# Two-layer convolution kernel: the low parts of x1 shared by GpSimd and VectorE, key sums moved ahead of the lane products, two x1 loads of the last stage issued earlier

## The reference, cut to what matters

```
layer 0: keys, queries, values = 1x1 convolutions of x
         context = softmax(keys over pixels) @ values ;  x1 = Wp(context, softmax(queries)) + x
layer 1: qkv  = w_qkv @ x1                       (768 channels = 32 heads x (q, k, v) x 8)
         agg  = 5x5 depthwise, then 8x8 pointwise convolution of qkv
         for both qkv and agg, per head:  q = relu(q), k = relu(k), v1 = [v, 1]
             vk  = v1 @ k^T over the pixels (9 x 8) ;  out = vk @ q ;  out = out[:8] / out[8]
         y    = w_proj @ out
         out  = batchnorm(y over all 8 images) * gamma + beta + x1
```

## Time and profile before

| | us |
|---|---|
| median of 3 runs | 2250.73 (2247.62 to 2252.7) |
| the profiled execution | 2251.85 |
| its span | 2250.1 |
| PE / DVE / ACT / POOL busy | 2059.1 / 1423.8 / 867.5 / 646.4 |
| layer 1 ends, last stage begins | 2146.3 |
| last stage | 103.8 |

### The profile page before, as it was taken

How to read it: one execution, slowest core, us unless ns; L and a number is a source line. 1 busy time by engine, 2 the same in 40 slices (tenths; PEclk the granted TensorE clock), 3 DMA queues, 4 the chain that set the end, 5 groups by cost and what they waited for, 6 DMA issues and landing times. The chain is left out here.

```text
span 2250.1 us, 33698 instructions
## 1 busy us (share of the span) xinstructions
PE 2059.1 (92%) x13448; PEld 1517.5 (67%) x13448; DVE 1423.8 (63%) x2052; ACT 867.5 (39%) x1841; POOL 646.4 (29%) x511
## 2 busy tenths in 40 slices
PE   8999999999897999999999999999999999999810
PEld 7888898888774666666666666766766666666500
DVE  6667776677248765948667575684857659480452
ACT  5444544444443423423433342343334234234142
POOL 1223312231324422522522242252243226221000
PEclk9999999999998999999999999999999999999855
DMA  3220122210677756764865776586486667647588
GB/s 124 85 85 17 69 85 85 85 74 12 232 268 267 250 199 239 261 225 172 288 230 203 266 265 210 194 292 216 167 303 237 209 238 252 228 172 263 237 340 373
DMA packets 144475, 450.91 MB, mean 200 GB/s; under 512 B 7744, under 2 KB 106688, under 8 KB 120000
## 3 DMA queue, kind: packets, MB, share of 16 engines
q1 hardware_dynamic: 143168, 429.89, 53.6%
q10 hardware_dynamic: 1152, 18.87, 2.0%
HBM read 273.95 MB, written 174.78 MB: 199 GB/s over the span
## 5 line engine op out<-in xcount | busy, mean ns | idle before, releaser
L791 PE MATMUL cv<-work,wc 128*64 128x288 f32 x4608 | 622.3, 415 | 15.9 <-issue 12.0
L1153 POOL TENSOR_TENSOR wc<-taps 128x512 f32<-128x512 f32 x288 | 366.3, 1299 | 499.4 <-PE cv L791 492.0
L791 PEld LDWEIGHTS cv<-work,wc 128*64 128x64 f32 x4608 | 308.3, 137 | 258.9 <-issue 51.5
L1233 DVE SCALAR_TENSOR_TENSOR spun<-work,spun 128x1152 f32<-128x1152 f32 x240 | 379.0, 1584 | 0.0
L1227 DVE STREAM_SHUFFLE spun<-work 128x1152 f32<-128x1152 f32 x240 | 347.9, 1456 | 0.1
L1015 ACT ACTIVATE work<-cv 128x288 f32<-128x288 f32 x384 | 157.6, 410 | 475.3 <-PE cv L791 473.6
L770 PE MATMUL pj<-x1hi,w1hi 128*128 128x288 f32 x768 | 237.3, 309 | 29.2 <-issue 24.3
L993 ACT COPY work<-pj 128x288 f32<-128x288 f32 x384 | 154.1, 401 | 232.4 <-PE pj L772 232.4
L772 PE MATMUL pj<-x1hi,w1lo 128*128 128x288 f32 x768 | 230.2, 300 | 0.0
L771 PE MATMUL pj<-x1lo,w1hi 128*128 128x288 f32 x768 | 229.0, 298 | 0.0
L420 POOL TENSOR_TENSOR qs<-qs,qrc 128x512 f32<-128x512 f32 x72 | 75.2, 1049 | 402.1 <-DVE qrc L474 402.1
(11 more groups left out here) (128 smaller groups left out, 3406.0 us busy)
## 6 DMA issues: line engine op xcount, KB each, us to landing
work<-scratch_padded SPq DMA_DIRECT2D x48, 1306.0 KB, 6.9
scratch_padded<-work SPq DMA_DIRECT2D x48, 1300.0 KB, 6.2
work<-scratch_padded SPq DMA_DIRECT2D x48, 1299.5 KB, 9.9
scratch_phases<-work SPq DMA_DIRECT2D x96, 576.0 KB, 4.6
work<-scratch_phases SPq DMA_DIRECT2D x64, 576.0 KB, 5.4
x<-scratch_x SPq DMA_DIRECT2D x9, 2304.0 KB, 11.2
scratch_x<-xs SPq DMA_DIRECT2D x8, 2304.0 KB, 6.9
q<-scratch_phases SPq DMA_DIRECT2D x32, 576.0 KB, 5.5
```

Source lines behind the costliest of these rows:

```text
L791: mm = nc.tensor.matmul(cv[64 * b:64 * b + 64, j % 2, :PLANE], wc[:, 2 * j + b, dy].rearrange("p c o -> p (c o)"), window, start=(dy == 0) ...
L1153: op = nc.gpsimd.tensor_tensor(wc[:, blocks, dy], taps[:, u % 2, blocks, 0:DIM].rearrange("p g (c o) -> p g c o", o=1).to_broadcast([P, HB ...
L1233: nc.vector.scalar_tensor_tensor(out=spun[:, t % 2], in0=kc[:, piece], scalar=1.0, in1=spun[:, t % 2], op0=ALU.mult, op1=ALU.mult, accum_o ...
```

## The change

Four edits:

1. `low` pieces 0 and 1 stay on POOL; pieces 2 and 3 go to DVE, after the third and after the fourth lane product of product 3. The semaphore `xlo_ready` becomes two, `xlo_front` and `xlo_back`. POOL makes both halves of unit 5's weights in a row.
2. The sum of the keys leaves the end of `spin` for a function `total`: for product 1 straight ahead of the spin, for product 3 ahead of the last piece of statistics. `total` waits for the keys alone, `spin` for the values alone.
3. The tile `xb` (x1 of images 2 and 3 in the last stage) is put over the weight, taps and `spun` tiles of layer 1, and its two loads are issued with the early ones at the end of layer 1.
4. For that, the early list has a fourth entry (without its y load) and the last stage's SP loop starts one later.

```diff
@@ phase_l1, sync @@
             for n, (y, x, loaded) in enumerate(early):
-                sp.dma_start(y, dram["y"][n]).then_inc(loaded, 16)
-                if x is not None:
-                    sp.dma_start(x, dram["x1"][n]).then_inc(loaded, 16)
+                if n < len(early) - 1:
+                    sp.dma_start(y, dram["y"][n]).then_inc(loaded, 16)
+                sp.dma_start(x, dram["x1"][n]).then_inc(loaded, 16)
@@ phase_l1, tensor: project @@
-                        pe.wait_ge(xlo_ready, 4 * i + c // 2 + 1)
+                        pe.wait_ge(xlo_front if c < 4 else xlo_back, 2 * i + c // 2 % 2 + 1)
@@ phase_l1, gpsimd @@
                     low(i + 1, [0, 1])
-                weights(i, 5, [0])
-                if i != last_image:
-                    low(i + 1, [2, 3])
-                weights(i, 5, [1])
+                weights(i, 5)
@@ phase_l1, vector @@
+            def total(i, p):
+                u = PRODUCTS[p][0] + PARTS.index(1)
+                for h in range(2):
+                    dve.wait_ge(lay_done[u % 2][h], laid_at(i, u))
+                wait_count(dve, dsel_ready, 4 * (i - 1) + p + 1)
+                nc.vector.tensor_reduce(vkd[:, p // 2, DIM:DIM + 1], kva[:, 0], AX.X, ALU.add)
...
                 if share[-1] == 15:
-                    wait_count(dve, dsel_ready, 4 * (i - 1) + p + 1)
-                    nc.vector.tensor_reduce(vkd[:, p // 2, DIM:DIM + 1], kc, AX.X, ALU.add)
                     dve.wait_ge(spun_summed, first + 16)
...
+                total(i, 1)
                 spin(i, 1, range(0, 6))
...
                     statistics(i - 1, Y_CHUNKS[2])
+                if i != last_image:
+                    total(i, 3)
                 if prev:
                     statistics(i - 1, Y_CHUNKS[3])
                 if i != last_image:
-                    spin(i, 3, range(0, 16))
+                    spin(i, 3, range(0, 3))
+                    low(i + 1, [2])
+                    spin(i, 3, range(3, 4))
+                    low(i + 1, [3])
+                    spin(i, 3, range(4, 16))
@@ phase_out, sync @@
                 if k >= NB:
                     sp.wait_ge(store[k % NB], 16 * (k // NB))
+                sp.dma_start(y, dram["y"][order[k]]).then_inc(loaded, 16)
                 if k > len(early):
-                    sp.dma_start(y, dram["y"][order[k]]).then_inc(loaded, 16)
-                sp.dma_start(x, dram["x1"][order[k]]).then_inc(loaded, 16)
+                    sp.dma_start(x, dram["x1"][order[k]]).then_inc(loaded, 16)
```

More of the change, by code:

```diff
@@ L543, in phase_l1 @@
         wlo = sb("w1lo", [P, CT, NU, P], F32R)
-        wproj = sb("wproj", [P, 4, C])
         taps = sb("taps", [P, 2, NB, DIM + KROWS * NG])
         wc = sb("wc", [P, NB, KROWS, DIM, NG])
+        spun = sb("spun", [P, 2, SPIN])
+        wproj = sb("wproj", [P, 4, C])
         ident = sb("ident1", [P, P])
@@ L564, in phase_l1 @@
         rlo = sb("rlo", [P, 2, CHUNK], F32R)
-        spun = sb("spun", [P, 2, SPIN])
         sums = sb("sums", [P, 2, DIM])
@@ L586, in phase_l1 @@
         rep_in = [sem(f"l1_rep_in{r}") for r in range(3)]
-        w_split, w_rest, xhi_ready, xlo_ready = sem("l1_w_split"), sem("l1_w_rest"), sem("l1_xhi_ready"), sem("l1_xlo_ready")
+        w_split, w_rest, xhi_ready = sem("l1_w_split"), sem("l1_w_rest"), sem("l1_xhi_ready")
+        xlo_front, xlo_back = sem("l1_xlo_front"), sem("l1_xlo_back")
         lay_stored, lay_done = ((lay_stored0, lay_stored1), (lay_stored2, lay_stored3)), ((lay_done0, lay_done1), (lay_done2, lay_done3))
@@ L1173, in low @@
                     nc.gpsimd.tensor_tensor(x_part(xlo, s), x_part(x1, s), x_part(xhi, s).bitcast(F32),
-                                            ALU.subtract).then_inc(xlo_ready, 1)
+                                            ALU.subtract).then_inc(xlo_front, 1)
             weights(0, 0)
@@ L1206, in _, with low @@
             nc.vector.tensor_tensor(wlo[:, :, 0:2], wqkv[:, :, 0:2], whi[:, :, 0:2].bitcast(F32), ALU.subtract).then_inc(w_split, 1)
[L1208 to L1211, removed]
+            def low(i, parts):
+                for s in parts:
+                    dve.wait_ge(xhi_ready, 4 * i + s + 1)
+                    nc.vector.tensor_tensor(x_part(xlo, s), x_part(x1 if i else x1_first, s), x_part(xhi, s).bitcast(F32),
+                                            ALU.subtract).then_inc(xlo_front if s < 2 else xlo_back, 1)
+            low(0, range(4))
             dve.wait_ge(w_rest, 1)
             nc.vector.tensor_tensor(wlo[:, :, 2:], wqkv[:, :, 2:], whi[:, :, 2:].bitcast(F32), ALU.subtract).then_inc(w_rest, 1)
+            def total(i, p):
[4 more added lines that the diff above has]
+                nc.vector.tensor_reduce(vkd[:, p // 2, DIM:DIM + 1], kva[:, 0], AX.X, ALU.add)
             def spin(i, p, share):
@@ L1219, in spin @@
                 if share[0] == 0:
-                    for u in (PRODUCTS[p][0], PRODUCTS[p][0] + 1):
-                        for h in range(2):
-                            dve.wait_ge(lay_done[u % 2][h], laid_at(i, u))
+                    for h in range(2):
+                        dve.wait_ge(lay_done[(PRODUCTS[p][0] + 1) % 2][h], laid_at(i, PRODUCTS[p][0] + 1))
                 def turn(t):
@@ L1308, in sb @@
             return ctx.enter_context(nc.sbuf_tensor(name, shape, F32))
-        xb = sb("xb", [P, 2, CT, HW])
+        sb("early_x", [P, 2, CT, HW])
         gb = sb("gb", [P, 2, CT])
@@ L1318, in phase_out @@
         sh = sb("sh", [P, CT])
-        g_in, stat, root, load0, load4, scaled, summed, store0, store1, store2, store3, store4 = (
+        g_in, stat, root, load0, scaled, summed, store0, store1, store2, store3, store4 = (
             sem(f"out_{n}") for n in
-            "g_in stat root load0 load4 scaled summed store0 store1 store2 store3 store4".split())
-        y_third, _, load3 = early[2]
-        buffers = ((q[:, 2:4, :], x1[:], load0), *early[:2], (y_third, xb[:, 0], load3), (q[:, 0:2, :], xb[:, 1], load4))
+            "g_in stat root load0 scaled summed store0 store1 store2 store3 store4".split())
+        buffers = ((q[:, 2:4, :], x1[:], load0), *early)
         store = (store0, store1, store2, store3, store4)
@@ L1420, in build @@
         parts = cut(work, *[(CT, HW)] * 4)
+        xb = nc.alloc_sbuf_tensor_at("xb", [P, 2, CT, HW], F32, offset=-(-nc.sbuf_base // 32) * 32)
         early = ((parts[0], parts[1], sem("out_load1")), (parts[2], parts[3], sem("out_load2")),
-                 (y_third[:], None, sem("out_load3")))
+                 (y_third[:], xb[:, 0], sem("out_load3")), (q[:, 0:2, :], xb[:, 1], sem("out_load4")))
         phase_l1(nc, dram, sem, bnst, q, x1, xhi, xlo, work, early, x_again, ahead, x_stored)
```

## The result

The changed kernel takes **2219.16 us** (median of 4 runs, 2217.31 to 2220.08); the kernel before took 2250.84 in 4 runs beside it. The ratio is 0.9856, with a 95% interval of 0.9843 to 0.9868. The prediction was 2228.6 with a range of 2220 to 2238. So the sign was right, and the gain is 31.7 us where 22.1 were forecast, just outside the range.

What follows compares the result with a forecast made beforehand. PE bounds layer 1, full DMA engines the last stage. Savings 2.5 (first hand-over) + 12.8 - 1.8 (six others) + 2.5 (image 0) + 3.8 (clock) + 2.3 (last stage) = 22.1 us, giving 2228.6 us, range 2220 to 2238.

Steps and rivals of the forecast that it cites:

- The bound and the places: Layer 1: PE sets the pace; its 24.3 us of projection stalls are waits for low pieces 2 and 3.
- The steady hand-overs: Six later hand-overs to a next image: 12.8 us saved at the projection, less 1.8 us for waits at turn_product.
- laid out by the rule it ends 1.3 us earlier: DVE's chain to vkm in steady images, with DVE and POOL taking turns: 1.3 us earlier.
- the working: DVE's chain per image: reduction 2.5 off, low pieces 2.6 on, waits about 2.0 + 1.0 off, shorter waits about 1.5 on.
- The clock: PE's clock behind hand-over stalls: three falls fewer of five, 1.27 us each, 3.8 us saved.
- rival 2: Hand-overs: no clock fall at all and DVE's piece 3 gets ahead of POOL; 2225 us, chance 15%.
- Image 0: Image 0: the keys' reduction moves into DVE's idle time, the whole chain comes earlier; 2.5 us saved.
- The first hand-over: Hand-over from image 0: piece 3 ends 1.5 us before its use, all 2.5 us of stalls go.
- The last stage: Last stage: first store gets the DMA engines alone, ends 5 us earlier, last load lands 2.3 us earlier; 2.3 us saved.
- the bound of 11 us: Last stage: upper bound of the saving, the full time of the two xb loads moved out, 11 us.
- 1.9 us a hand-over: Steady hand-overs: PE's gain limited to DVE's 1.3 us earlier end plus 0.56 us slack.
- Rivals 1, 3, 4 and 5: Falls all stay, 2231, 25%; POOL two turns per DVE's, 2239, 13%; only image 0, 2248, 3%; late statistics, slower, 2%.

Runs made afterwards that it cites:

- the late use of vkm: Changed kernel with turn_product and project_product of product 3 one group later on PE and ACT; 2217.89 us, ratio 0.9853.
- the last two kernels: Changed kernel with DVE's low pieces in a row, late vkm use, image 0's unit 4 weights and x1 load earlier: 2206.91; first hand-over's low pieces all on POOL: 2204.67.

## Why the prediction was partly wrong

**The bound and the places: right.** The two stalls at the projection were waits for low pieces 2 and 3. The stall for piece 2 went, one for piece 3 stayed, vkm became the next wait, and the sum on its own is worth nothing in a steady image.

**The steady hand-overs: the mechanism right, the size off.** Predicted were 11.0 us (12.8 - 1.8), measured 16.4, that is 2.73 instead of 1.83 each. The step that failed is "laid out by the rule it ends 1.3 us earlier". DVE's chain ended 2.19 us earlier (50.40 to 48.21). Of its terms the reduction was right: 50.54 to 48.21 is 2.33 against 2.5. The low pieces were not: net +1.1 in the working, +0.14 in the run with them alone. The term at fault is what the lane products no longer wait for. The working had 3.0 us, for the two products that meet POOL's last two low pieces. Beyond the 1.34 us of an undisturbed one, the sixteen products take 8.0 us more in all in the kernel before (image from 904.61) and 4.1 in the changed one, so 3.9 went: later products run freer too. The two low pieces took 4.4 (2.21 each), where the working had 2.6 + 1.5 = 4.1. I had laid out the turns of DVE and POOL up to piece 3 and summed up the rest. The run with both low pieces in a row, which does the same work and is 1.27 us longer, shows that such a sum is no better than about 1 us, and six hand-overs multiply it. With PE's slack of 0.5 us the chain allows 2.7, which is what was measured. The stall for piece 3 was 0.91 us instead of 1.5, but PE would have waited for vkm instead of it, so this miss alone moves nothing.

**The clock: predicted 3.8, measured 6.4.** I had no row for a single stall of 1.5 us and took three falls of five. The stall measured 0.91 us, and the runs show no fall behind any single wait of 0.9 us. Behind one of 1.5 us none was tried; single waits of 1.77 us did drop the clock in the run with the early loads alone. So the low forecast came from the too long stall, and whether three of five would have been right for 1.5 us stays open; rival 2 had this part right ("no fall at all"). What the prediction had not seen is that a wait for vkm of 2.5 us would have brought the falls back: with the low pieces alone, where DVE's chain is no shorter, the time is 2250.18, so without a shorter chain the change would have been worth little more than its last stage and image 0.

**Image 0: predicted 2.5, measured 3.2.** Vkm begins 697.54 - 695.05 = 2.5 us earlier, as laid out, and so does the x1 load. The rest is the load itself, whose end comes 3.2 us earlier (ACT's high piece begins at 710.41 instead of 713.60). Up to this point the kernels scatter: 714.4 to 717.3 in the four with the sum in its old place, 710.2 to 714.3 in the eight with the moved sum and otherwise the old image 0. So this term is not known to better than 1 us. PE's wait fell by 3.8 us (to 8.1), not by 2.6: it ends 2.5 us earlier, as laid out, and began 1.3 us later. Behind it the clock is low for a while in both kernels. Behind the next wait (3.83 us before, 3.82 now, for ACT) it was low in the kernel before and at 2.4 GHz in the changed one. The windows are the kernel before, then the changed kernel:

```profile
714.80:720.00 5.20, 4.80 (x19) 2.34 (x21) 5.16 (x5) 3.42 (x7) 5.17 (x2) 0.50 0.46 130
```

```profile
711.60:716.80 5.20, 4.79 (x37) 2.67 (x37) 5.20 (x4) 3.92 (x8) 5.16 (x2) 1.00 0.52 146
```

Nothing in the change explains this difference: two waits of the same length, one with a fall and one without.

**The first hand-over: predicted 2.5, measured 3.25**, from other terms than mine. The stalls fell from 2.5 to 0.28 us, as laid out. The clock was at full at its start, where the kernel before had 0.50 (the windows above); what that is worth was not separated. A wait of 1.84 us for a DMA (`scratch_padded`) is new in this execution. No other run has it there, also none of those with the early loads. In the run without them the distance is 185.5 instead of 186.5, and with them and the late use of vkm it is 185.8. Why the wait appears was not tried.

**The last stage: predicted 2.3, measured 3.5.** The mechanism, a first store that has the DMA engines for itself, is what happened. It ends 5.1 us earlier in the stage (21.6 us behind its start instead of 26.7), as laid out. The step that was mis-sized comes behind it: the layout let 2.3 of these 5 us reach the last load, measured are 3.4 (the store that waits for it is issued 83.4 us into the stage, at 2200.30, instead of 86.8, at 2233.13). Which of the queues' turns the layout had wrong was not looked into. The second load is worth nothing; the bound of 11 us was far off, and rightly not taken.

**The rivals.** Rival 2 (no fall, 2225) named the right branch for the clock and was bounded by the same wrong 1.9 us a hand-over; with 2.73 it would have said 2225 - 6 x 0.83 = 2220. Rivals 1, 3, 4 and 5 didn't happen. The statistics started on time, and the sum found its keys.

## What to carry to other kernels

Behind the stall that an edit removes, find the next wait of the same engine and lay out its chain with the same care, to its end: here the next wait ate one edit wholly (0.07% alone) and the edit that shortened its chain was worth nothing alone either (0.1%), while both gave 1.36%. Where two engines take turns on one resource, a layout by turns must go on to the instruction that somebody waits for; here the sum made by hand behind the first few turns missed by 1 us an image. And after any such edit look at where PE's longest single wait now stands, since the clock's fall can move with it.

## What the runs showed of the hardware

- In layer 1's hand-overs a single PE wait of 0.9 or 1.28 us never dropped TensorE's clock (36 of 36), nor did the one of 1.84 and the one of 2.15. Single waits of 1.76 or 1.77 us dropped it to 1.2 GHz five times in one execution, before a second wait began. Waits of 2.5 us dropped it in 9 of 12, and two waits close together (1.75 and 1.89 us in most) were followed or parted by a fall in 19 of 21.
- Equal waits went different ways: 2.57 and 2.53 us in one execution, and 3.83 and 3.82 us in image 0 of the kernel before (a fall) and of the changed kernel (none). The four waits of 3.4 to 5.0 us in image 0 of the last two kernels each came with a fall.
- One fall costs 1.27 us behind the projection's stalls (191.18 - 189.91), 1.7 us behind the wait for vkm (190.1 - 188.4), and nothing where the slower PE only used up a wait that came next (189.91 with a fall, in the run with the early loads alone).
- DVE and POOL, taking turns at SBUF, do the same work in times that differ by 1.27 us (48.21 and 49.48 from low piece to vkm), by the order of two of DVE's instructions alone: it takes PE's stall of 0.91 us away, so POOL's next weights start 1.1 us earlier against DVE.
- A low piece on DVE takes 1.35 us alone, 2.21 beside POOL's weights; on POOL it is 2.65, and 3.77 beside the products. Two of them moved to DVE lengthened its chain by 0.14 us.
- The first store of the last stage takes 7.0 us with no load in its way and 12.1 beside loads.
